# Writing out the loops of a gated recurrence and moving the feed-forward block's side work to earlier units

## The reference, cut to what matters

```python
x = x + attention(layernorm(x))          # 16 heads, 8 segments, rotary positions
x = x + ffn(layernorm(x), w_up, w_down)  # 256 -> 1024 -> 256, ternary weights
x = x + recurrence(layernorm(x))         # 16 heads of 16, 512 steps
x = x + ffn(layernorm(x), w_up, w_down)

def ternary_linear(x, w):                # used twice in ffn, exact gelu between
    x_norm = x / (rms(x) + 1e-8)         # rms over the features of a row
    return x_norm @ ternary(w).T

def step(state, inp):                    # state: batch x head x 16 x 16
    r, k, v, w, a, kk = inp
    sa = sum_j(state * -kk)
    state = w * state + sa * (kk * a) + k * v
    norm = sqrt(mean_j(state * state))
    state = state / (norm + 1e-5)
    return state, sum_j(state * r)
```

## Time and profile before

| | us |
|---|---|
| median of 3 runs | 2644.86 (2641.38 to 2644.88) |
| the profiled execution, its own time | 2637.25 |
| its span, first to last instruction | 2634.0 |
| DVE busy | 2193.4 (83%) |
| PE busy | 1948.5 (74%) |
| ACT busy | 1612.9 (61%) |
| POOL busy | 907.4 (34%) |

### The profile page before, as it was taken

How to read it: one execution, slowest core, us unless ns; L and a number is a source line. 1 busy time by engine, 2 the same in 40 slices (tenths; PEclk the granted TensorE clock), 3 DMA queues, 4 the chain that set the end, 5 groups by cost and what they waited for, 6 DMA issues and landing times.

```text
span 2634.0 us, 52211 instructions
## 1 busy us (share of the span) xinstructions
PE 1948.5 (74%) x12353; PEld 1563.6 (59%) x12353; DVE 2193.4 (83%) x8801; ACT 1612.9 (61%) x5207; POOL 907.4 (34%) x1522
## 2 busy tenths in 40 slices
PE   5888887788688768777768787777886764345687
PEld 3555554445577767677667676677776763233454
DVE  6888777687239999999999999999999999992576
ACT  4888777566355565556666666666665554443566
POOL 0000000111025555555555555555555555550111
PEclk7999899899887787687887778877777776665799
DMA  5001000000000000000000000000000000000000
GB/s 170 16 20 27 20 16 12 1 1 1 1 0 1 1 1 1 1 1 1 1 1 1 1 1 1 1 1 1 0 0 1 1 1 1 1 1 0 9 25 33
DMA packets 14327, 24.52 MB, mean 9 GB/s; under 512 B 1280, under 2 KB 12032, under 8 KB 13824
## 3 DMA queue, kind: packets, MB, share of 16 engines
q1 hardware_dynamic: 14080, 21.97, 2.9%
HBM read 12.27 MB, written 4.19 MB: 6 GB/s over the span
## 4 chain that ended last, share of the span: by engine, by line
DVE 53%; issue 21%; PE 17%; ACT 8%; DVEq 1%; DMA 0%; POOL 0%; SPq 0%; ACTq 0%; POOLq 0%
DVE pn L1447 11%; DVE bank L1463 10%; DVE U L1504 7%; DVE xs L1435 4%; DVE bank L1452 4%; DVE kv L1496 4%; PE bank L248 3%; ACT prob L828 3%; PE bank L543 2%; PE bank L260 2%; PE bank L590 1%; DVE bank L1493 1%; DVE bank L1472 1%; PE bank L770 1%; PE bank L692 1%
## 5 line engine op out<-in xcount | busy, mean ns | idle before, releaser
L1581 POOL TENSOR_TENSOR wu<-U,stg 128x256 f32<-128x256 f32 x512 | 317.7, 620 | 761.3 <-DVE U L1504 761.3
L707 PE MATMUL bank<-U,ident 128*128 128x128 f32 x2080 | 470.3, 398 | 86.4 <-ACT go L969 72.0
L707 PEld LDWEIGHTS bank<-U,ident 128*128 128x128 f32 x2080 | 432.5, 235 | 124.5 <-issue 51.5
L770 PE MATMUL bank<-stack,tm 128*128 128x64 f32 x1792 | 325.3, 365 | 183.4 <-ACT tm L906 183.2
L770 PEld LDWEIGHTS bank<-stack,tm 128*128 128x128 f32 x1792 | 314.3, 276 | 204.2 <-issue 204.2
L1108 ACT ACTIVATE xs<-U 128x128 f32<-128x128 f32 x1024 | 262.3, 302 | 261.5 <-DVE U L1504 258.7
L1447 DVE TENSOR_REDUCE pn<-xs 128x16 f32<-128x256 f32 x1024 | 377.7, 409 | 7.3 <-issue 6.7
L1036 ACT ACTIVATE small<-pn 128x16 f32<-128x16 f32 x513 | 110.9, 216 | 371.3 <-DVE pn L1447 371.3
L1537 POOL TENSOR_TENSOR kv<-stg 128x256 f32<-128x256 f32 x513 | 317.4, 619 | 0.0
L1435 DVE TENSOR_TENSOR xs<-U,bank 128x128 f32<-128x128 f32 x1024 | 243.2, 278 | 67.6 <-issue 66.9
L1463 DVE TENSOR_TENSOR bank<-wu,bank 128x128 f32<-128x128 f32 x1024 | 292.2, 286 | 1.0 <-POOL wu L1581 0.7
(11 more groups left out here) (180 smaller groups left out, 3722.4 us busy)
## 6 DMA issues: line engine op xcount, KB each, us to landing
out_x<-x SPq DMA_DIRECT2D x8, 512.0 KB, 2.9
x<-in_x SPq DMA_DIRECT2D x1, 3584.0 KB, 16.9
Vs<-V SPq DMA_DIRECT2D x8, 384.0 KB, 4.6
Vs<-V SPq DMA_DIRECT2D x8, 288.0 KB, 3.3
lane<-in_lanes SPq DMA_DIRECT2D x8, 256.0 KB, 3.3
wcat<-in_wcat SPq DMA_DIRECT2D x1, 1792.0 KB, 14.0
wraw<-in_w_up SPq DMA_DIRECT2D x1, 1024.0 KB, 19.0
wraw<-in_w_down SPq DMA_DIRECT2D x1, 1024.0 KB, 11.4
```

The source lines that it names most:

```text
L707: last = pe.matmul(rsum.rearrange("p (t i) -> p t i", i=HD), ident[:, :], steps[:, :, :, j], start=(j == 0), stop=(j == HD - 1))
L770: last = pe.matmul(bank[3 + g][:, e * CH:(e + 1) * CH], tm[:, g * (PB // 2) + e, :, :].rearrange("p a c -> p (a c)"), stack[:, :], start=T ...
L1581: pool.tensor_tensor(ij(wu[:, :]), ij(U[:, half if j else 1 - half, (j - 1) % STEPS, :]), col(stg[:, half, j, TW, :]), ALU.mult).then_inc( ...
```

## The change

There are two parts. The first takes every `Fori` out of the recurrence, its prologue and its tail, on PE, ACT, DVE and POOL: the loop variable becomes a Python number, so all passes are written out, and step counts and row numbers that were computed in registers (`snap`) become constants. The arithmetic instructions and their order stay. The second part reorders the feed-forward block. For the next group q+1, `row_scales` and all four `rows_normalised` now stand in unit 0 (were units 2 and 3), the transposes in units 2 and 3 (were 4, 5), `split_high` in 3 and 4 (were 5, 6), `split_low` in 4 and 5 (were 6, 7). The statistics are taken one group further ahead: those of q+2 in units 1 to 3 of group q, and those of the second group before unit 0 (in block 0 within the last batch of attention). `add_rows` spreads over units 4 to 6 (was 4, 5), and bank 1 comes before bank 0 in transposes and splits.

```diff
                 if q >= 2:
-                    pe.wait_ge(F["sr"], q if q % B == 0 else q - 1)
-                    pe.wait_ge(F["lo"], (q - 1) * KD + k + 1)
+                    pe.wait_ge(F["sr"], q if q % B == 0 else q - 1 if k == 0 else q - 2)
+                    pe.wait_ge(F["lo"], q * KD - k)
...
                 pe.wait_ge(A["x2"], B * NT)
-            for k in range(KD):
+            for k in (1, 0):
...
                         square_sums(q - 1)
-                    if n in (4, 5) and q < i * B + B - 1:
-                        rows_transposed(q + 1, n - 4)
+                    if n in (2, 3) and q < i * B + B - 1:
+                        rows_transposed(q + 1, 3 - n)
...
             def split_high(q, k):
-                act.wait_ge(F["xt"], q * KD + k + 1)
+                act.wait_ge(F["xt"], q * KD + 2 - k)
...
-            for k in range(KD):
+            for k in (1, 0):
...
                     act.activation(hsq[:, t % 2, :], h[:, t % 2, :], ACT.Square).then_inc(F["sq"], 1)
-                    if n in (5, 6) and q < i * B + B - 1:
-                        split_high(q + 1, n - 5)
-
-        def row_stats(dve, q):
+                    if n in (3, 4) and q < i * B + B - 1:
+                        split_high(q + 1, 4 - n)
+
+        def row_stats(dve, q, us=range(NT)):
...
             dve.wait_ge(F["xn"], q * NT)
-            for u in range(NT):
+            for u in us:
...
             def split_low(q, k):
-                dve.wait_ge(F["hi"], q * KD + k + 1)
+                dve.wait_ge(F["hi"], q * KD + 2 - k)
...
                 rows_normalised(dve, q0, range(NT))
-            for k in range(KD):
+            for k in (1, 0):
...
                 split_low(q0, k)
+            if not beside_first:
+                row_stats(dve, q0 + 1)
+                row_moments(dve, q0 + 1)
...
                         if n == 0:
-                            row_stats(dve, q + 1)
-                            row_moments(dve, q + 1)
-                        if n == 2:
...
                             row_scales(dve, q + 1)
-                        if n in (2, 3):
-                            rows_normalised(dve, q + 1, (2 * n - 4, 2 * n - 3))
-                        if n in (6, 7):
-                            split_low(q + 1, n - 6)
+                            rows_normalised(dve, q + 1, range(NT))
+                        if n in (4, 5):
+                            split_low(q + 1, 5 - n)
+                    if q + 1 < q9:
+                        if n in (1, 2):
+                            row_stats(dve, q + 2, (2 * n - 2, 2 * n - 1))
+                        if n == 3:
+                            row_moments(dve, q + 2)
...
                             output_scales(q - 1)
-                        if n in (4, 5):
-                            add_rows(q - 1, (2 * n - 8, 2 * n - 7))
+                        if n in (4, 5, 6):
+                            add_rows(q - 1, ((0,), (1, 2), (3,))[n - 4])
...
             row_roots(q0)
+            row_roots(q0 + 1)
...
             for q in range(q0, q9 + 1):
-                if q < q9:
-                    row_roots(q + 1)
...
                     output_roots(q - 1)
+                if q + 1 < q9:
+                    row_roots(q + 2)
...
                     pe.wait_ge(C["x1"], min(ot + 3, NT) * B)
-                with pe.Fori(0, NB // 2) as pair:
+                for pair in range(NB // 2):
...
                     act.wait_ge(O["t1c"], (2 * ot + 2) * NB)
-                with act.Fori(0, NB // 2) as pair:
+                for pair in range(NB // 2):
...
                         else:
-                            t0 = act.snap(n * CH + m * STEPS)
-                            it = act.snap(n * NB + m)
-                            row_it = act.snap(n % 2 * CH + m * STEPS)
-                            row_next = act.snap((n % 2 * CH + m * STEPS + STEPS) % (2 * CH))
+                            t0 = n * CH + m * STEPS
+                            it = n * NB + m
+                            row_it = n % 2 * CH + m * STEPS
+                            row_next = (n % 2 * CH + m * STEPS + STEPS) % (2 * CH)
...
                     rows_normalised(dve, 0, range(NT))
+                if w == 16:
+                    row_stats(dve, 1)
+                if w == 17:
+                    row_moments(dve, 1)
...
                 if not running:
-                    with dve.Fori(0, NB) as m:
+                    for m in range(NB):
...
                     continue
-                with dve.Fori(0, NB // 2) as pair:
+                for pair in range(NB // 2):
...
                         m = pair * 2 + half
-                        t0 = dve.snap(n * CH + m * STEPS)
-                        it = dve.snap(n * NB + m)
+                        t0 = n * CH + m * STEPS
+                        it = n * NB + m
...
                     pool.wait_ge(O["os"], (n - 1) * NB)
-                with pool.Fori(0, NB // 2) as pair:
+                for pair in range(NB // 2):
...
                         m = pair * 2 + half
-                        t0 = pool.snap(n * CH + m * STEPS)
-                        it = pool.snap(n * NB + m)
-                        row_next = pool.snap((n % 2 * CH + m * STEPS + STEPS) % (2 * CH))
-                        row_last = pool.snap((n % 2 * CH + m * STEPS + (2 * CH - STEPS)) % (2 * CH))
+                        t0 = n * CH + m * STEPS
+                        it = n * NB + m
+                        row_next = (n % 2 * CH + m * STEPS + STEPS) % (2 * CH)
+                        row_last = (n % 2 * CH + m * STEPS + (2 * CH - STEPS)) % (2 * CH)
```

## The result

The median of the changed kernel is **2526.53 us** (4 runs, 2524.28 to 2529.22), against 2643.12 us for the kernel before (4 runs, 2640.54 to 2644.88): ratio 0.956, 95% interval 0.9543 to 0.9577. The forecast was 2527 (2508 to 2570). Of all the runs in this document one execution fell into a slower state of the chip (2709.27 us at a granted clock of 0.657, in the kernel that leaves only DVE its loops), and it is left out. The profiled execution of the changed kernel took 2528.14 us, with a span of 2526.2.

What follows compares the result with a forecast made beforehand. DVE's own sequence was taken to bound the recurrence; in the feed-forward no engine was full and PE had a hole. -71 - 5 - 1.5 - 41 + 1.1 = -117.4 us on 2637.25 gives 2519.9; median forecast 2527 us (2508 to 2570).

Steps and rivals of the forecast that it cites:

- Term 1: Recurrence: writing out the loops removes 24 jumps back on DVE and their issue time, -71 us (60 to 75).
- lose their jumps too: Recurrence: ACT, POOL and PE jump at the same time as DVE and lose their jumps as well; no separate size.
- Rival C: Recurrence: a return costs only its branch, 0.35 us, the other issue time stays; gain 54 us, 2591 us, chance 0.04.
- Rival B: Written-out code arrives too slowly on four engines: 50 stretches at 2.9 us cost 145 us, 2673 us; chance 0.03.
- Term 2: Prologue and tail: jumps back removed by writing out the loops, -5 us and -1.5 us.
- the prologue's -5: Prologue, chunk -1, where PE and ACT alternate: three jumps of 1.66 us go, -5 us (3 to 5.5).
- the tail's -1.5: Tail: DVE's wait of 3.44 instead of 3.04 us at every second turn goes, -1.5 us (0.5 to 3).
- Term 3: Feed-forward: the reordering removes PE's hole of 2.58 us per group and keeps the clock up, -41 us (15 to 50).
- Units 4 and 5, the ones feared: Feed-forward groups: 2.7 us of DVE work in each of these units might open new holes, at the gain's low end, 15.
- +1.1 for the statistics: End of attention: block 0's second-group statistics, 2.09 us, stand behind `rdx` and delay oT_a, +1.1 us.
- The base taken: Whole kernel: the median of runs stands 7.6 us above the profiled execution's 2637.25 us.

Runs made afterwards that it cites:

- the two half cuts: Kernel before with only DVE's loops written out, 2563.93 us; kernel before with only the loops of PE, ACT and POOL written out, 2638.41 us.
- the cut with PE, ACT and POOL: Kernel before with the loops of PE, ACT and POOL written out while DVE keeps its loops: 2638.41 us, ratio 0.9998.

## Why the prediction was right, and where it was not

**Term 1 (-71): right in mechanism, 7 us too small.** The issue time of the earlier trace rows went from 73.6 to 0.3 us, 73.3 in all; I had kept 2.3 us of it as if it would stay. The other 5 us are no idle time: DVE's busy time over the stage fell by 4.2 us (1530.5 to 1526.3), and 1.2 us before U went. Around a return the overlap of two neighbouring instructions, about 0.1 us as in the rows of 860.24, is lost too, and a list of idle times does not show that; this would explain most of the 4.2, but no run tests it. The reading that code is fetched again after a jump back, and in chunk 5 is still at hand, is borne out by the packets. That ACT, POOL and PE "lose their jumps too" was worth nothing in the recurrence, as the two half cuts show, and they had no dear jumps to lose. Rival C's counter-argument, "chunk 5 has the same instructions", was sound: with another position chunk 5 pays the full price. Rival B took fresh code for the dear case. It is the returns that fetch most, five packets in a pass where one in sequence needs 2.7 (B counted it as 214 rows; it is 343 instructions). Written out, the four engines fetch 0.5 MB more than with loops, and no stall over 0.3 us stands in DVE's sequence: code in sequence arrives ahead of its use. The Trainium skill's 51 and 108 ns for the branches ("Advanced Engine Details and Errata", section Control Flow Timing) would have made the gain of the recurrence about 5 us, an estimate; it gained 78.

**Term 2: the prologue's -5 failed, the tail's -1.5 was small.** The failed step is "over a jump back 9.35 us ... Three jumps of 1.66 us". It read ACT's wait for PE as a jump, because it came in every second half, without a look at PE's rows for the same time. The matmuls are 1.7 us longer there, at the lower clock, and nothing is left of the 1.66 us for the jump. The other 0.08 us per half (7.69 against 7.61) stand in ACT's part, 1.27 against 1.19. Whether the jump helps to set off the lower clock stays open: before, it begins 1.3 us behind each of PE's four branches in this chunk, but the written-out kernels have such stretches too, fewer and longer. What the stage gains by it can't be told beforehand. With loops it took 93.0 to 93.6 us, written out 91.9 to 95.6 by the kernel around it (95.2 and 95.1 in the changed one). The tail gave 3.1 (2.4 in the cut with PE, ACT and POOL): PE and ACT alternate, and a turn became 4.57 us from a mean of 4.80.

**Term 3 (-41): right, -39.8.** Groups were put at 19.6 and 18.6 us. The middle ones are longer, 19.9 and 19.0, and the first of each block, at 18.1, which the prediction did not single out, makes up for it: the means of the seven are 19.5 and 18.8. The clock stayed at 2.4 GHz through idle times of up to 0.9 us inside a group. Units 4 and 5, the ones feared, do fill DVE without a gap, and that is what bounds a group now.

**+1.1 for the statistics: 0.5**, for the reason given above. **The sum** hit 2527 to 0.5 us partly by luck: 7 us more from term 1 and 1.6 from the tail stand against 6.5 us less from the prologue and 1.2 from term 3. The profiled pair, with an attention 10.6 us longer than forecast at a lower clock, gained only 109. The base taken, a median 7.6 us above the profiled execution, did stand for a common run: the attention of that execution, at 479.8 us, is the fastest seen.

## What to carry to other kernels

Where an engine waits for nothing but its own issue at the start of each pass of a loop, and the engine sets the pace, look whether the instruction queues move packets behind its branches, and write the loop out: a return cost 2.9 us here, code in sequence nothing. Do it first on that engine alone; the others here had shorter passes (up to 201 instructions on ACT and POOL, against 362 and more), fetched nothing on their returns and waited for DVE besides, so their loops cost nothing in the recurrence and keep the program short. A shorter pass on DVE, which might fit as theirs did, was not tried. Before a periodic delay is put down to a jump, compare the durations of the matmuls in it: a stretch at 1.2 GHz looks the same in the waits of the engine behind. And remove a hole of a few us on PE, or fill it, for the clock behind it as well: that was a third to a half of its price in a group where the clock fell.
